# Batch 0's prologue of attention: mixing of groups 2 and 3 moved, stacks copied in two parts, statistics moved into the attention loop

## The reference, cut to what matters

```python
x = x + 0.5 * _L0_ffn_ref(_layernorm(x), W_r, W_k, W_v, mu_r, mu_k)
x = x + _L0_attn_ref(_layernorm(x), qkv_w, qkv_b, proj_w, proj_b)
x = x + 0.5 * _L0_ffn_ref(_layernorm(x), W_r, W_k, W_v, mu_r, mu_k)
...                          # a mixture of experts, linear attention, again a mixture of experts
# _L0_ffn_ref ("mixing"): x_prev is x shifted by one token
xr = mu_r * x + (1 - mu_r) * x_prev;  xk = mu_k * x + (1 - mu_k) * x_prev
out = sigmoid(xr @ W_r.T) * (square(relu(xk @ W_k.T)) @ W_v.T)
# _L0_attn_ref: 16 heads of 8, rotary embedding on q and k
attn = softmax(q @ k.T * 8 ** -0.5);  out = (attn @ v) @ proj_w.T + proj_b
```

## Time and profile before

| | us |
|---|---|
| median of 3 executions | 1353.01 (1352.94 to 1354.49) |
| the profiled execution | 1355.71 |
| its span, first to last instruction | 1353.8 |
| PE busy | 1091.2 (81%) |
| DVE busy | 655.0 (48%) |
| ACT busy | 806.7 (60%) |
| POOL busy | 375.7 (28%) |
| mean granted clock of TensorE | 0.896 |

### The profile page before, as it was taken

How to read it: one execution, slowest core, us unless ns; L and a number is a source line. 1 busy time by engine, 2 the same in 40 slices (tenths; PEclk the granted TensorE clock), 3 DMA queues, 4 the chain that set the end, 5 groups by cost and what they waited for, 6 DMA issues and landing times.

```text
span 1353.8 us, 20967 instructions
## 1 busy us (share of the span) xinstructions
PE 1091.2 (81%) x7616; PEld 508.4 (38%) x7616; DVE 655.0 (48%) x2060; ACT 806.7 (60%) x1164; POOL 375.7 (28%) x376
## 2 busy tenths in 40 slices
PE   3459899989989999999879489877887777898940
PEld 2332222223222321232256356443544344565630
DVE  5742555464454340433165146567666662633522
ACT  4328778788887999989734345654443331364520
POOL 2100111112100102333002744144240363155535
PEclk8779989999999999999999789889788686898985
DMA  4450450450038301100012233100000011133522
GB/s 138 62 90 1 70 83 1 71 81 2 2 54 149 102 3 62 68 15 28 9 43 69 80 90 100 34 15 19 9 17 1 13 33 40 49 112 100 143 66 67
DMA packets 83411, 74.07 MB, mean 55 GB/s; under 512 B 11248, under 2 KB 77680, under 8 KB 82416
## 3 DMA queue, kind: packets, MB, share of 16 engines
q1 hardware_dynamic: 73824, 55.06, 18.8%
q0 software_dynamic: 8192, 16.79, 4.3%
q10 hardware_dynamic: 1296, 0.86, 0.2%
HBM read 39.26 MB, written 33.42 MB: 54 GB/s over the span
## 4 chain that ended last, share of the span: by engine, by line
PE 53%; DVE 20%; ACT 11%; issue 5%; POOL 3%; DMA 2%; another core or an unknown queue 1%; SPq 0%; POOLq 0%; DVEq 0%; ACTq 0%
PE ps L987 11%; PE ps L1659 9%; ACT attn_probs L1250 9%; PE ps L972 6%; PE ps L1685 4%; PE ps L590 3%; PE ps L881 2%; PE ps L1962 2%; PE ps L1671 2%; POOL moe_back L1604 2%; PE ps L1649 1%; PE ps L1886 1%; DVE lin_scores L2091 1%; DVE moe_xr L1105 1%; DVE room L1106 1%
## 5 line engine op out<-in xcount | busy, mean ns | idle before, releaser
L1250 ACT ACTIVATE attn_probs<-ps 128x1024 f32<-128x1024 f32 x512 | 486.1, 1083 | 91.3 <-PE ps L972 91.2
L987 PE MATMUL ps<-attn_probs,attn_v 128*18 128x512 f32 x2048 | 275.1, 610 | 1.9 <-DVE room L1217 1.3
L972 PE MATMUL ps<-stack 50*128 50x512 bf16 x1024 | 167.3, 391 | 17.6 <-DMA stack<-row_maxima 11.5
L1594 POOL DMA_INDIRECT slots<-moe_xr,moe_slot x128 | 124.9, 975 | 197.5 <-ACT attn_probs L1250 78.9
L1659 PE MATMUL ps<-stack,lin_scores 128*128 x312 | 155.4, 621 | 0.0
L1604 POOL DMA_INDIRECT moe_back<-results,moe_slot x128 | 123.6, 966 | 111.0 <-PE ps L1649 47.2
L972 PEld LDWEIGHTS ps<-stack 50*128 50x128 bf16 x1024 | 34.3, 94 | 255.5 <-ACT attn_probs L1250 228.8
L1760 ACT ACTIVATE lin_scores<-ps 128x256 f32<-128x256 f32 x156 | 58.4, 381 | 105.6 <-PE ps L1659 100.3
L1733 DVE TENSOR_TENSOR lin_scores<-ps,lin_scores 128x256 f32<-128x256 f32 x156 | 59.1, 419 | 105.0 <-ACT lin_scores L1760 85.3
L1685 PE MATMUL ps<-stack,lin_scores 128*128 x624 | 86.6, 283 | 10.3 <-ACT lin_heads_out L1773 6.8
L1685 PEld LDWEIGHTS ps<-stack,lin_scores 128*128 128x128 f32 x624 | 78.7, 198 | 12.2 <-issue 11.9
(11 more groups left out here) (237 smaller groups left out, 1584.4 us busy)
## 6 DMA issues: line engine op xcount, KB each, us to landing
stack<-qk_parts SPq DMA_DIRECT2D x48, 256.0 KB, 9.2
moe_gathered<-slots SPq DMA_DIRECT2D x76, 128.0 KB
results<-lin_heads_out SPq DMA_DIRECT2D x76, 128.0 KB
slots<-zeros SPq DMA_DIRECT2D x2, 2496.0 KB, 14.9
qk_parts<-moe_xr SPq DMA_DIRECT2D x32, 128.0 KB, 5.2
qk_parts<-moe_xr SPq DMA_DIRECT2D x16, 192.0 KB, 2.8
stack<-in_expert_w SPq DMA_DIRECT2D x1, 3072.0 KB
x<-in_x SPq DMA_DIRECT2D x8, 256.0 KB, 8.4
```

The source lines that it names most:

```text
L972: instruction = T.matmul(k.ps[:, SCORE_BANKS[i % 3][s], :], d.stack[b % 2][rows, 1, pair, kt * P:(kt + 1) * P], d.stack[b % 2][rows, 0, pa ...
L987: instruction = T.matmul(k.ps[32 * j:32 * j + STRIP, PV_BANK, :], d.v[:, b % 2, kt, first:first + STRIP], d.probs[:, n % A_PROBS, j * BANK ...
L1250: A.activation(d.probs[:, n % A_PROBS, 2 * e * BANK:2 * (e + 1) * BANK], k.ps[:, banks[0]:banks[1] + 1, :].rearrange("p a n -> p (a n)"), ...
L1594: G.indirect_dma_start(out=k.dram["slots"][half], out_offset=bass.IndirectOffsetOnAxis(ap=d.slot[:, s, at, c:c + 1], axis=0), in_=d.xr[:, ...
```

## The change

- `weights` moves behind the normalisations of groups 0 and 1.
- The statistics of groups 4 to 7 leave the prologue and become side work of attention, with factors for each batch of their own (`x_factors`).
- In `k.start`, batch 0's queries and both maxima pieces come without other work in between. Then comes a new piece `max_in`, then `mn` of groups 2 and 3, the values, and the rest of the mixing. The statistics of the mixed groups 2 and 3 (`mixed`) and their factors become side work of attention's first steps.
- For batch 0, ScalarE issues the maxima's write (behind `max`) and its two loads (at `max_in`, after waiting for the write); SyncE did. For batches 1 to 3 SyncE still does.
- Batch 0's stacks are copied in two parts: pairs 0 and 1 of queries and keys with a semaphore of their own, `a_stack_first`, then pairs 2 to 7. Both come after all parts have been written. Scores of the first pair group wait for the first, those of the second for the rest. 24 copies take the place of 12.
- TensorE waits for the cleared PV bank only before the first weighted sums. ScalarE waits for `mv` of group 3 before step 1 and for the additions before step 2.
- Values of batches 1 to 3 begin at step 7 of the batch before instead of step 3.

```diff
 def plan_start(k):
-    k.start = [("x_stats", 0), ("x_stats", 1), ("factors", 0, TPB), ("weights",), ("mn", 0), ("mn", 1), ("mt", 0), ("mt", 1),
+    k.start = [("x_stats", 0), ("x_stats", 1), ("factors", 0, TPB), ("mn", 0), ("mn", 1), ("weights",), ("mt", 0), ("mt", 1),
                ("x_stats", 2), ("x_stats", 3), ("mk", 0), ("mr", 0), ("mk", 1), ("mr", 1), ("mv", 0), ("mv", 1), ("ms", 0), ("ms", 1),
                ("factors", 0, 2 * TPB)]
-    side = [(kind, g) for kinds in (("mn",), ("mt",), ("mk", "mr"), ("mv",), ("ms",)) for g in (2, 3) for kind in kinds]
-    later = [("x_stats", g) for g in range(4, GROUPS)]
-    for _, piece in attention_queries(0):
-        k.start.append(piece)
-        if piece[0] == "norms" and later:
-            k.start.append(later.pop(0))
-        elif piece[0] == "split":
-            k.start.append(side.pop(0))
-    bound, shift = [piece for _, piece in attention_maxima(0)]
-    k.start += [bound] + side[:2] + [piece for _, piece in attention_values(0)] + [shift] + side[2:]
-    k.start += [("factors", TPB, TILES)]
+    k.start += [piece for _, piece in attention_queries(0)] + [piece for _, piece in attention_maxima(0)]
+    k.start += [("max_in",), ("mn", 2), ("mn", 3)] + [piece for _, piece in attention_values(0)]
+    k.start += [(kind, g) for kinds in (("mt",), ("mk", "mr"), ("mv",)) for g in (2, 3) for kind in kinds]
 def plan_attention(k):
-    begin = {0: [list(attention_queries(1)) + list(attention_maxima(1))]}
+    begin = {0: [[(OTHER, ("mixed", 2)), (OTHER, ("mixed", 3)), (OTHER, ("factors", TPB, 2 * TPB))]
+                 + list(attention_queries(1)) + list(attention_maxima(1))]}
     for b in range(2, BATCH):
         mixed = ("factors", b * TPB, (b + 1) * TPB)
-        begin.setdefault(FIRST_AT[b], []).append(side_mixes(2 * b - FIRST_MIXES, 2 * b - FIRST_MIXES + 2) + [(OTHER, mixed)])
+        work = [(OTHER, ("x_stats", 2 * b)), (OTHER, ("x_stats", 2 * b + 1)), (OTHER, ("x_factors", b * TPB, (b + 1) * TPB))]
+        begin.setdefault(FIRST_AT[b], []).append(work + side_mixes(2 * b - FIRST_MIXES, 2 * b - FIRST_MIXES + 2) + [(OTHER, mixed)])
     for b in range(1, BATCH):
-        begin.setdefault(STEPS_PER_BATCH * (b - 1) + A_LAG + 1, []).append(list(attention_values(b)))
+        begin.setdefault(STEPS_PER_BATCH * (b - 1) + VALUES_AT, []).append(list(attention_values(b)))
...
 def scores(n, b, half, group, kt):
         if group == half == kt == 0:
-            T.wait_ge(k.a_stack_in[b % 2], STACK_IN * (b // 2 + 1))
+            if b == 0:
+                T.wait_ge(k.a_stack_first, STACK_IN)
+            else:
+                T.wait_ge(k.a_stack_in[b % 2], STACK_IN * (b // 2 + 1))
             T.wait_ge(k.a_max_in, 32 * (b + 1))
+        if b == half == kt == 0 and group == 1:
+            T.wait_ge(k.a_stack_in[0], STACK_IN)
...
 def act_start(A, k):
         act_mix(A, k, piece)
+        if piece == ("max", 0):
+            maxima_out(A, k, 0)
+        if piece == ("max_in",):
+            maxima_in(A, k, 0)
 def act_attention(A, k):
-    A.wait_ge(k.mix_added, FIRST_MIXES)
+    gated_bank, gated_n = k.use["mv", 0, FIRST_MIXES - 1]
     for n in range(len(A_STEPS) + A_LAG):
+        if n == 1:
+            A.wait_ge(k.free[gated_bank], gated_n + 1)
+        if n == 2:
+            A.wait_ge(k.mix_added, FIRST_MIXES)
+def maxima_out(E, k, b):
+    bank, n = k.use["max", b]
+    E.wait_ge(k.free[bank], n + 1)
+    E.dma_start(k.dram["maxima"][b].rearrange("k r q -> r k q"), k.attn.max_parts[:, :, :]).then_inc(k.a_max_out, 16)
+def maxima_in(E, k, b):
+    d = k.attn
+    E.wait_ge(k.a_max_out, 16 * (b + 1))
+    for s in range(2):
+        row = s * STACK + QK_ROWS
+        source = k.dram["maxima"][b].rearrange("k (r s j) q -> s k r (j q)", s=2, j=TPB)[s]
+        E.dma_start(d.stack[b % 2][row:row + MAX_ROWS, 0, :, :], source).then_inc(k.a_max_in, 16)
 def sp_attention(S, k, expert_w):
             write_parts(b, i)
-            if half:
+            if half and b:
...
+        if b == 0:
+            for qk in range(2):
+                parts_landed(b, 2 * qk + 1)
+                stack_parts(b, qk, slice(0, 2), k.a_stack_first)
+            for qk in range(2):
+                stack_parts(b, qk, slice(2, PAIRS), k.a_stack_in[0])
+        if b:
+            maxima_out(S, k, b)
+            maxima_in(S, k, b)
```

More of the change, by code:

```diff
@@ L303, in plan_attention @@
         for work in begin.get(n, []):
-            works.insert(len(works) if work[0][1][0] in ("norm", "factors", "mn") else 0, work)
+            works.insert(len(works) if work[0][1][0] in ("norm", "mixed", "x_stats", "factors", "mn") else 0, work)
         out = turn_of(works)
@@ L785, in side @@
         kind, j = piece[0], piece[1] if len(piece) > 1 else None
-        if kind == "factors":
+        if kind == "x_stats":
+            dve_mix(V, k, piece)
+        elif kind == "mixed":
+            dve_mix(V, k, ("ms", j))
+        elif kind in ("factors", "x_factors"):
             dve_norm_factors(V, k, slice(piece[1], piece[2]))
@@ L1345, in stack_parts, with parts_landed @@
                 rows = slice(s * STACK + 16 * row, s * STACK + 16 * (row + 1))
-                S.dma_start(d.stack[b % 2][rows, qk, :, :].rearrange("p r t -> p (r t)"),
-                            source).then_inc(k.a_stack_in[b % 2], 16)
+                cols = slice(pairs.start * SEQ, pairs.stop * SEQ)
+                S.dma_start(d.stack[b % 2][rows, qk, :, :].rearrange("p r t -> p (r t)")[:, cols],
+                            source[:, cols]).then_inc(done, 16)
+    def parts_landed(b, i):
+        for other in range(2):
+            S.wait_ge(k.a_parts_out[other], parts_out(b, i) + PARTS_OUT[i // HALVES])
     S.wait_ge(k.a_blank, 4)
@@ L1356, in sp_attention @@
             write_parts(b, i)
[L1357 to L1359 removed]
+            if half and b:
+                parts_landed(b, i)
                 if b >= 2:
                     S.wait_ge(k.a_score, 2 * STEPS_PER_BATCH * (b - 1))
[L1362 to L1370 removed]
+                stack_parts(b, qk, slice(0, PAIRS), k.a_stack_in[b % 2])
+        if b == 0:
+            for qk in range(2):
[6 more added lines that the diff above has]
+            maxima_in(S, k, b)
     zero = k.zeros[:, :][:, None, :].broadcast_to([P, SLOT_TILES, DIM])
```

20 lines of the change are left out of this document (6 added, 14 removed).

## The result

| | before | after |
|---|---|---|
| median | 1354.49 (1351.45 to 1361.36, 15 executions) | 1359.48 (1353.33 to 1367.40, 15 executions) |
| ratio | | 1.0040, 95% interval 1.0022 to 1.0057 |
| profiled execution, its span | 1355.71, 1353.8 | 1363.59, 1361.8 |
| first exponential | 96.51 | 85.13 |
| start of the last step (its first exponential) | 664.0 | 677.0 |

The change makes the kernel 5.0 us slower, where 9.3 us less were forecast. The start did what the prediction said, nearly to a tenth: the first exponential runs 11.4 us earlier (11.3 forecast). Then attention, from the start of its first step to the start of its last, takes 24.4 us longer: 677.0 - 85.1 = 591.9 where it took 664.0 - 96.5 = 567.5. Forecast was 2.0.

What follows compares the result with a forecast made beforehand. Attention is paced by ScalarE's exponentials, after a serial prologue until 96.51 set by the queued row-maxima transfer. Gain 11.3 - 1.5 - 0.5 = 9.3 us, off the median 1343.7; range 1339.5 to 1351.5.

Steps and rivals of the forecast that it cites:

- Weights, queries, bound: Prologue: weights 0.8 and VectorE work off the queries 6.8 us earlier; keys' last rounding about 60.4, shift ready 64.0.
- Issue and landing: Row maxima before attention: issued at 66.0, landed 3.5 us later at 69.5, loads back issued until 71.0.
- the quiet row: Profile row of a 64 KB transfer landing in 2.3 us with little else under way; a bound for the maxima's landing.
- Mixing behind the wait: Prologue's end: copy and transposes until 72.7, mixing 11.7 us until 84.4, first exponential at 85.2.
- Rival 1: The maxima's round trip costs as much as now, landing in 11.7 us: 1351.9, chance 0.08.
- Stacks in two parts: Batch 0's 24 copies: first quarter lands by 78, rest by about 90, before step 8 wants it; cost nothing.
- Start of attention, net 1.5: First steps: VectorE's 10.9 us queue stalls TensorE some 3.6, but the start stalled before too; net loss 1.5 us.
- Later 0.5: Attention near step 48: statistics of groups 6 and 7 and factors find VectorE between rotations; 0.5 us (0 to 4.9).
- their number doesn't change: Attention's side products: three later turns move to the tail, where steps have none, their number the same; no loss given.
- Rival 3: VectorE pays in attention: half of 14.7 us, 1349.1, chance 0.15; all of it, 1356.4, chance 0.05.
- Rival 4: The new order shrinks batch 1's 4.20 us ScalarE stall by about 3: 1340.7, chance 0.10.

Runs made afterwards that it cites:

- the order alone: The old order with empty turns where the change inserts work and values at step 7, so no moved VectorE work there; 1356.13 us, ratio 1.0009.
- the old order: Changed kernel with attention's side work at its steps before the change, input statistics in the prologue, mixed statistics before the first side piece; 1345.81 us, ratio 0.9951.
- the work alone: The old order with all moved VectorE work inside attention, before the first side piece and at steps 45 to 47; 1354.23 us, ratio 1.0001.
- values at 7: The old order with the values of batches 1 to 3 from step 7 of the batch before instead of 3; 1334.51 us, ratio 0.9965.

## Why the prediction was wrong

- **Weights, queries, bound: right in sum** (the parts were not measured one by one). Last keys' rounding at 59.91 (60.4 forecast, 66.82 before), shift ready at 63.37 + 0.29 = 63.7 (64.0).
- **Issue and landing: right.** Issued at 66.01 (66.0). Landed in 2.6 us instead of 3.5, as by the quiet row, loads issued by 70.4 (71.0).
- **Mixing behind the wait: right.** Copies over at 72.5 (72.7), last step of VectorE's mixing at 84.1 (84.4), so 11.6 us for the 11.7. First exponential 85.13 (85.2). Rival 1 did not occur.
- **Stacks in two parts, "cost nothing": right, but understated.** No stall of step 8 is in the trace. What the text did not see is that the split is what lets the maxima pass: without it they took 25.1 us and the ratio is 1.0121. Of the two sections that the prediction cited from the Trainium skill, DMA: Bandwidth & Descriptors, the first, "Issuing engines are not separate DMA queues", agrees with the landing: 1.9 us from SyncE and 2.6 from ScalarE. The second, "Queues, rings and completion order", has each engine take turns between queues packet by packet. The trace with whole stacks agrees in the turns (205 packets of the write beside 96 large ones from 77 to 90 us), but not in what the prediction drew from it, that the maxima pass after a few stack packets: they are many small packets, each turn of the other queue costs about 2.1 us, and the turns began only ten microseconds after the issue.
- **Start of attention, net 1.5: too small.** The stall came where it was put and was as long (3.68 on TensorE against 3.6), but the net loss by step 8 was 3.6 us: 5.45 and 1.39 of idle came in the place of 2.48 and 0.45. The 1.5 does not follow from its terms either: 3.6 less the old stall of 2.48 is 1.1. The queue that it counted as 10.9 adds up to 10.8, and took 96.68 - 85.83 = 10.85.
- **"Later 0.5" and "their number doesn't change": wrong, and this is the step that failed.** I counted the inserted turns as work to be added up and priced their order at nothing, and the values at step 7 too (2.4 us at most). Measured: 20.8 us after step 8. The step was that a list shifted by three turns goes through the same pieces. It does, but it then meets divisions, sum copies and values at fixed steps, and pieces that had been spread over steps 67 to 81 pile up on VectorE in 76 to 84. The kernel with the order alone loses the same microseconds in the same steps, 19.0 of 19.1 from step 64 on. The late statistics near step 48, to which the 0.5 was given, cost nothing where they were tried in the old order.
- **Rival 3** had the right place and nearly the right size, all of the 14.7 us paid (1356.4 from the three executions' median of 1353.0; measured 1359.5 beside 1354.5), but not the mechanism, so that its number came near is luck: with the work and without the order, attention is 4.8 us longer than with neither (576.5 against 571.7). **Rival 4**, that the new order helps, had the right suspect with the wrong sign: for one stall in batch 1, read from the earlier trace rows, it did not look at what the same shift does to batch 2.

Attention's 24.4 us, by kernels that start within 2 us of each other: 4.2 come with the early start itself (old order, 571.7 against 567.5), which uncovers the mixed groups' statistics, 11.9 with the order alone (583.6), 4.8 with the work alone (576.5), and 3.5 only with both together. The 11.9 are a net: from step 64 on the order costs 19.0, and before that the empty turns win 7.0, because the statistics are done by the time their results are wanted.

The old order beats both kernels: 8.4 us below the kernel before, 14.6 below the changed one. Still open: why the medians show only 5.0 and 5.2 of the 13 us by which attention ends later. Both profiled executions of the change lie above their medians, by 4.1 and 6.9 us, and on the chip of the second profile the rest of the program took 691.5 us in it against 689.8 in the old order, so that the stages behind attention take less in the changed kernel is not shown. How an execution at the median splits its time no run shows.

## What to carry to other kernels

Where side work is walked one turn a step beside pieces at fixed steps, an inserted turn is a change of order for everything behind it: lay both orders out step by step over the whole stage and add up each engine's work between the fixed pieces, rather than adding up the moved work. Idle time in the total (VectorE 49% busy after) says nothing of four steps in which it is a serial queue with TensorE behind it. A small transfer on the way to a stage's start should be issued, out and back, before the bulk, and the copies ahead of it should be small; with small ones ahead, which engine issued it was of little weight here.

## What the runs showed of the hardware

- A 64 KB write (256 packets of 256 bytes) from ScalarE's queue landed in 2.6 us beside stack copies of 64 KB each, in packets of 4 KB, and in 25.1 us beside copies of 256 KB, in packets of 16 KB. Of these 25.1 us, ten passed with nothing of it served, and in the next 13 some two of its packets ran for each large one. Before, on SyncE's queue behind copies of 256 KB, it took 11.7. From SyncE's queue behind twelve copies of 64 KB: 1.9 us.
- Loads back issued at 68.59 were landed before the first score at 84.63; those issued at 70.65, behind the first large copies, landed some 19 us later, at 90. Issued at 69.27, 0.1 us behind the first large copy (values at 7), the first score product did not wait for them.
- The 54 us behind attention, with the same code, ran at a granted clock of 0.87 in some kernels and 0.91, 0.94 or 0.97 in others, and the rest of the program took 684.8 to 695.3 us in these executions (three chips; 671.7 to 673.7 on a fourth). That is a scatter of the order of what this change was to bring; the step times inside attention repeat far better (591.9 and 591.9 us for the change on two chips, 409.1 us for steps 64 to 255 in both kernels with the old order).
- A stall cost more than its wait: TensorE idled 3.50 us until 297.57, its granted clock was 1.00 before and 0.50 from 298 to 304, and in steps 80 to 83 it was 0.77 on average where it was 1.00 in the old order; 67 products were busy for 11.5 us where 70 took 8.8.
